# The attention mask moves from a TensorE product to a GpSimd addition, and the one-element copy in front of VectorE's score step goes

## The chip, the cores and the metric

One Trainium2 chip, one of its cores. The metric is the device time of one execution in microseconds (us). The engines are called PE (TensorE, with PEld for its weight loads), DVE (VectorE), ACT (ScalarE), POOL (GpSimd) and SP (SyncE, which here only issues transfers).

## The reference

Sixteen sequences (a batch each) of 512 tokens with 512 features pass through a chain: a finite-difference step on a 512x512 field, then a transformer layer, then an adapter with two 2x2 rotations. Only the transformer layer matters here, and of it the attention:

```python
scores = jnp.einsum('bhqd,bhkd->bhqk', q / math.sqrt(HEAD_DIM), k)
scores = scores + attention_bias
scores = jnp.where(src_mask, -jnp.inf, scores.astype(jnp.float32))
probs = jax.nn.softmax(scores, axis=-1).astype(v.dtype)
ctx = jnp.einsum('bhqk,bhkd->bhqd', probs, v)
```

There are 16 heads of 32 features. The bias is 16 x 16 x 512 x 512 float32 (268 MB in all) and is read once; the mask is one byte per query and key, the same for all heads of a batch. After the attention come the output product, a layer norm, a feed-forward part with 2048 hidden units, and the adapter.

## The kernel before

**Tiles and stages.** The kernel goes through the 16 batches one after the other. Within a batch the attention works in four groups g = 0..3. A group holds four heads (HG = 4) and all four blocks of 128 queries (TB = 4), so it has 16 score blocks of 128 queries by 512 keys, numbered i = 4q + j. A score block i of a group lives in `prob[:, i, :]` from the landing of its bias to its turn. All products with large matrices are split into high and low parts in float32r; the low part of a weight is computed by POOL (`split_lo`, line 628) from the raw weight and the high part that ACT copied (`split_hi`, line 689), and PE waits for it through `w_lo`.

**One score block.** PE multiplies query and key parts into one of two PSUM banks (L915), and a second matmul with a bfloat16 identity adds the mask rows `mask_add` to the same bank (L916). DVE copies one element (`fence`, L1117; that instruction carries the waits for the scores and for the bias in `prob`), and then one custom instruction computes score plus bias negated into `prob` with its row minimum into `low` (L1118). ACT takes the exponential and the row sum (L698). PE turns the block in four 128x128 pieces (L927), ACT copies the turned block to `probT` (L719), and PE multiplies every four of them with V (L950).

**Order of the work.** Every engine has its order written out by hand. Iteration i of a group on PE issues the score block i + 7 (`S_LEAD` = 7, running over into the next group), then turns block i, then some pieces of the query and key product for the group after the next (`qk_piece`, L891; in groups 0 and 1 from i = 5 on), and at i = 1, 5, 9, 13 the product with V. ACT takes in iteration i the exponential of block i + 6 (`EXP_LEAD` = 6), then the copy of block i; at i = 14 of a group this is the exponential of block 4 of the next group. DVE takes the score step i + 7 and, in the first four iterations, the steps that make the next group's query and key: L1098 and L1096 (from PSUM to `wide`) and the two L1103 (low parts: `wide` minus `parts`, both in SBUF).

**SP's queue** decides when transfers start. In each of groups 0 to 2, SP issues after the turns of blocks 1 and 3 two bias loads for the next group (each 512 KB: two blocks of `prob`, `load_bias`, L531). It then waits for both L1103 (`qk_lo`) and issues the 16 small transfers that lay out query and key for the next group (`load_stack`, L536). Only then come the bias loads for blocks 4 to 15 of the next group, each after the turn of the second block whose place it takes. PE's score block 0..3 of the next group (iterations 9 to 12) waits for its four `load_stack` transfers. In the feed-forward part, SP loads weight chunks and, between them, the bias of the next batch's group 0.

**POOL's queue** before the change: per batch 24 low parts of weights (L628), three additions of a bias row to 128x2048 tiles (L650 in group 0, L664, L676) and 12 small roots (L633). In the attention it holds few instructions: in group 0 the low part for group 2's weights and then L650, at the start of group 1 the low part for group 3's weights, at the start of group 2 that of the first half of the output weights, in group 3 that of their second half.

**The feed-forward part** goes over 16 chunks f. For each one PE makes the hidden units (12 matmuls), ACT applies the activation into `gel` (L810) and copies the high part (L814), DVE makes the low part (L1197, both inputs in SBUF), and PE makes the second product (12 matmuls) after the first product of the next chunk. At f = 8, 10, 12 and 14 DVE also scales a quarter of the next input in `adapt`: L1067, L1080 and L1081, each waiting for the one in front of it. ACT makes the high part of chunk f + 3 at the end of its chunk f, and POOL follows with the low part.

Of the kernel before, what the change touches and what calls it, by code (L numbers as in the profile page):

```python
# [18 lines left out]
BF16 = mybir.dt.bfloat16  # L19
U8 = mybir.dt.uint8  # L20
I32 = mybir.dt.int32
ALU = mybir.AluOpType
# [390 lines left out]
def layers(nc, keep, x1, mask, bias, ada_rows, sel_turned, Wq, bq, Wk, bk, Wv, bv, Wo, bo, W1, b1, W2, b2, g2, beta2,  # L413
# [3 lines left out]
    with ExitStack() as ctx:  # L417
# [19 lines left out]
        mask_eye = sb("mask_eye", [P, P], BF16)  # L437
# [41 lines left out]
        eye_ready, score_full, scored, exped, inv_ready, inverted = (  # L479
            sem(n) for n in ("eye_ready", "score_full", "scored", "exped", "inv_ready", "inverted"))  # L480
# [21 lines left out]
        with nc.Block() as block:  # L502

            @block.sync
            def _(sp):
                for signal in (*w_hi, *w_lo, *proj_full, *proj_read, probT_full, tok_ready, mask_ready, mixed, ff2_done,
                               pv_done, g_lo, turn_lo, scored, *turned_copied, ctx_scaled, out_ready):
                    sp.sem_inc(signal, START)
# [112 lines left out]
            def _(pool):  # L621
# [13 lines left out]
                pool.wait_ge(keep["ident_in"], 16)  # L635
                pool.tensor_copy(mask_eye[:], ident[:]).then_inc(eye_ready, 1)
# [6 lines left out]

                pool.wait_ge(consts_in, 16 * 12)
                for b in range(0, B):
# [5 lines left out]
                    for g in (1, 2):  # L651
                        split_lo(0, ITEMS[0] * b + W0_QK + g + 2)
# [13 lines left out]

                    for f in range(6, NF):
                        split_lo(*chunk_item(b, f // 4, f % 4))
                        if more and f < 6 + TB:
                            root(ROOTS * b + 2 * TB + f - 5, f - 6)  # L670
# [169 lines left out]
            def _(t):  # L840
# [68 lines left out]
                def score_block(b, g, i):  # L909
# [5 lines left out]
                    t.matmul(score[i % 2][:], stack[g % 2][:, j, 0, q * P:(q + 1) * P], stack[g % 2][:, j, 1, :], start=True, stop=False)  # L915
                    t.matmul(score[i % 2][:], mask_eye[:], mask_add[:, q, :], start=False, stop=True).then_inc(score_full, 1)  # L916
# [55 lines left out]
                t.wait_ge(eye_ready, 1)  # L972
# [3 lines left out]
                for b in range(0, B):  # L976
                    t.wait_ge(mask_ready, b + 1 + START)
# [76 lines left out]
            def _(v):  # L1054
# [14 lines left out]
                def number_mask(b):  # L1069

                    v.wait_ge(mask_in, 16 * (b + 1))
                    v.tensor_scalar(mask_add[:], mask8[:], MASKED, None, ALU.mult).then_inc(mask_ready, 1)
# [39 lines left out]
                def score_step(b, g, i):  # L1112

                    v.wait_ge(score_full, 64 * b + 16 * g + i + 1)
                    if i % 2 == 0:
                        v.wait_ge(bias_in[i // HG][i % HG // 2], 16 * (4 * b + g + 1))
                    v.tensor_copy(fence[:, i % 7:i % 7 + 1], cur[:, 0:1])  # L1117
# [219 lines left out]
```

## Time and profile before

| what | before |
|---|---|
| time, median of 3 runs | 4866.53 us (4855.59 to 4870.71) |
| profiled execution | 4863.62 us, of it a span of 4861.2 us between first and last instruction |
| busy in the span | PE 88%, PEld 63%, DVE 54%, ACT 51%, POOL 26% |
| mean granted TensorE clock | 0.945 of full speed |
| moved by DMA | 704.31 MB, mean 145 GB/s |

In the rows below, a timeline row gives the start, the duration, the engine, the line of the kernel, the operation, written and read tile names, shapes and count; what stands in square brackets is the idle time of that engine just before the row and what ended it. A group row (by line) gives busy time and the mean duration of one, then the idle time before them. A duration of an instruction that had to wait after it was issued holds that wait too. In the windows, what follows the stretch and its length is the busy time (and instructions) of PE, PEld, DVE, ACT and POOL, then the granted TensorE clock, the DMA share and GB/s. Batches are counted from 0. L12 is line 12 of the kernel before.

### The profile page before, as it was taken

How to read it: one execution, taken by the hardware profiler on the slowest of the kernel's cores; microseconds unless marked ns; L12 is line 12 of the kernel's file. 1: busy time of each engine (PE TensorE's matmuls, PEld its weight loads, DVE VectorE, ACT ScalarE, POOL GpSimd, SP SyncE). 2: the span in 40 equal slices, each digit the busy share in tenths (PEclk: the TensorE clock that was granted, in tenths of full speed). 3: DMA queues.
4: the chain of work that ended last, by engine and by line, in shares of the span. 5: the costliest groups of instructions: out<-in, count | busy, mean ns of one | idle time of the engine just before them, and what ended most of it. 6: DMA issues, size and time to landing. Idle time of an engine off the chain costs nothing.

```text
span 4861.2 us, 70568 instructions
## 1 busy us (share of the span) xinstructions
PE 4253.7 (88%) x25568; PEld 3038.8 (63%) x25808; DVE 2612.4 (54%) x5783; ACT 2489.6 (51%) x4700; POOL 1272.4 (26%) x637
## 2 busy tenths in 40 slices
PE   6996688898989898888989898888989898988887
PEld 3441466676767666666767676666767676666665
DVE  8991545545463646455454646455454636455553
ACT  0002464737474555647374655647374746546472
POOL 0000132231414232231414142332314142322313
PEclk9995899999999999999999999999999999999999
DMA  3223653636364554536364644536363645545361
GB/s 120 105 97 67 200 172 106 192 109 183 124 195 132 162 164 118 178 105 193 115 182 136 188 144 138 169 107 191 109 183 124 195 132 162 163 113 182 108 181 48
DMA packets 534759, 704.31 MB, mean 145 GB/s; under 512 B 45280, under 2 KB 254992, under 8 KB 534384
## 3 DMA queue, kind: packets, MB, share of 16 engines
q1 hardware_dynamic: 517520, 666.23, 46.2%
q10 hardware_dynamic: 16896, 33.56, 1.8%
q8 instruction: 209, 3.42, 0.3%
q14 instruction: 134, 1.10, 0.1%
HBM read 529.30 MB, written 35.72 MB: 116 GB/s over the span
## 4 chain that ended last, share of the span: by engine, by line
PE 54%; DVE 12%; SPq 7%; ACT 6%; issue 5%; DMA 3%; POOL 3%; another core or an unknown queue 0%; POOLq 0%; DVEq 0%; ACTq 0%
PE bank L846 33%; SPq L536 7%; PE bank L891 5%; PE bank L927 5%; PE bank L915 3%; PE bank L950 3%; DVE prob L1118 2%; PE bank L916 2%; DMA stack<-parts 2%; DVE parts L1197 1%; ACT probT L719 1%; DMA V<-in_L_cond_W 1%; DVE parts L1103 1%; ACT prob L698 1%; PE bank L855 1%
## 5 line engine op out<-in xcount | busy, mean ns | idle before, releaser
L628 POOL TENSOR_TENSOR w<-w_raw,w 128x1024 fp32r<-128x1024 f32 x240 | 587.7, 2449 | 2067.0 <-ACT w L689 1935.7
L698 ACT ACTIVATE prob<-prob,low 128x512 f32<-128x512 f32 x1024 | 736.6, 719 | 171.8 <-DVE low L1118 171.8
L1197 DVE TENSOR_TENSOR parts<-gel,parts 128x512 fp32r<-128x512 f32 x256 | 261.3, 1021 | 893.7 <-ACT parts L814 893.7
L719 ACT ACTIVATE probT<-bank 128x512 f32<-128x512 f32 x1024 | 608.8, 595 | 248.7 <-PE bank L927 234.0
L927 PE MATMUL bank<-ident,prob 128*128 128x128 f32 x4096 | 641.1, 280 | 96.3 <-ACT probT L719 70.4
L1118 DVE CUSTOM_DVE_ANT_0 prob<-bank,prob 128x512 f32<-128x512 f32 x1024 | 696.3, 680 | 0.0
L927 PEld LDWEIGHTS bank<-ident,prob 128*128 128x128 f32 x4096 | 504.2, 145 | 204.3 <-issue 77.8
L915 PE MATMUL bank<-stack 128*128 128x512 f32 x1024 | 485.5, 476 | 105.0 <-DMA stack<-parts 58.2
L1117 DVE COPY fence<-cur 128x1 f32<-128x1 f32 x1024 | 155.5, 152 | 676.8 <-PE bank L916 334.9
L846 PE MATMUL bank<-xT,stack 128*128 128x512 f32 x1920 | 491.5, 405 | 23.1 <-DVE xT L1089 12.0
L628 POOL TENSOR_TENSOR stack<-V,stack 128x1024 fp32r<-128x1024 f32 x144 | 353.0, 2454 | 596.2 <-ACT stack L689 592.5
L891 PE MATMUL bank<-xT,w 128*128 128x512 f32 x1152 | 421.9, 469 | 62.5 <-POOL w L628 62.5
L846 PEld LDWEIGHTS bank<-xT,stack 128*128 128x128 f32 x1920 | 361.1, 192 | 138.6 <-DVE xT L1089 32.4
L810 ACT ACTIVATE gel<-bank,b_col 128x512 f32<-128x512 f32 x256 | 176.5, 690 | 505.7 <-PE bank L846 505.7
L846 PE MATMUL bank<-xT,w 128*128 128x512 f32 x1536 | 379.7, 396 | 0.0
L689 ACT ACTIVATE w<-w_raw 128x1024 fp32r<-128x1024 f32 x240 | 253.9, 1058 | 244.7 <-PE bank L846 222.1
L846 PE MATMUL bank<-w,parts 128*128 128x512 f32 x1536 | 372.1, 393 | 6.3 <-DVE parts L1197 6.3
L846 PE MATMUL bank<-stack,parts 128*128 128x512 f32 x1536 | 373.5, 392 | 0.0
L846 PE MATMUL bank<-w,xT 128*128 128x512 f32 x1536 | 369.4, 398 | 1.9
L846 PEld LDWEIGHTS bank<-w,parts 128*128 128x128 f32 x1536 | 287.0, 188 | 77.6 <-DVE parts L1197 13.3
L846 PEld LDWEIGHTS bank<-w,xT 128*128 128x128 f32 x1536 | 286.0, 188 | 78.8 <-DVE xT L1129 8.9
L846 PEld LDWEIGHTS bank<-xT,w 128*128 128x128 f32 x1536 | 288.1, 188 | 68.7
(182 smaller groups left out, 5881.9 us busy)
## 6 DMA issues: line engine op xcount, KB each, us to landing
prob<-in_fside_Bx16xSxS SPq DMA_DIRECT2D x512, 512.0 KB, 4.9
stack<-parts SPq DMA_DIRECT2D x1024, 128.0 KB, 2.5
V<-in_L_cond_W SPq DMA_DIRECT2D x256, 256.0 KB, 3.7
w_raw<-in_L_cond_W SPq DMA_DIRECT2D x256, 256.0 KB, 3.0
field<-in_x SPq DMA_DIRECT2D x16, 1024.0 KB, 5.3
x<-total ACTq DMA_DIRECT2D x16, 1024.0 KB, 5.9
xin<-x SPq DMA_DIRECT2D x16, 1024.0 KB, 5.6
w_raw<-in_L_cond_Wv SPq DMA_DIRECT2D x64, 256.0 KB, 2.9
```

What stands on the lines that cost most here:

```text
L536: sp.dma_start(stack[g % 2][DH * quad:DH * (quad + 1), j, :, :].bitcast(F32), parts[DH * j:DH * (j + 1), q:q + step + 1:step, :].bitcast(F ...
L628: pool.tensor_tensor(w[s][:, 1, :], w_raw[s], w[s][:, 0, :].bitcast(F32), ALU.subtract).then_inc(w_lo[s], 1)
L689: act.activation(w[s][:, 0, :], w_raw[s], ACT.Copy).then_inc(w_hi[s], 1)
L698: act.activation(prob[:, i, :], prob[:, i, :], ACT.Exp, bias=low[:, i:i + 1], scale=-1.0, accum_out=total[:, g % 2, i:i + 1]).then_inc(exp ...
L719: act.activation(probT[:, i % 8, :], turned[e % 2][:], ACT.Copy).then_inc(turned_copied[e % 2], 1)
L810: act.activation(gel[:, s, :], proj[s][:], ACT.Gelu_apprx_sigmoid, bias=col["b1"][:, f:f + 1]).then_inc(proj_read[s], 1)
L846: mm = t.matmul(dst, stat(hs, k), mov(hm, k), start=start and n == 0, stop=stop and n == count - 1)
L891: mm = t.matmul(proj[c][:], weight(0, hs)[:, KB * c + k, :], xT[hm][:, k, :], start=n == 0, stop=n == len(QK_TERMS) - 1)
L915: t.matmul(score[i % 2][:], stack[g % 2][:, j, 0, q * P:(q + 1) * P], stack[g % 2][:, j, 1, :], start=True, stop=False)
L927: mm = t.transpose(turned[e % 2][:, k * P:(k + 1) * P], prob[:, i, k * P:(k + 1) * P], ident[:])
L1118: v.tensor_tensor_reduce(prob[:, i, :], score[i % 2][:], prob[:, i, :], -1.0, MIN_START, ALU.add, ALU.min, low[:, i:i + 1]).then_inc(score ...
L1197: v.tensor_tensor(parts[:, 2 * (f % 2) + 1, :], gel[:, f % 2, :], parts[:, 2 * (f % 2), :].bitcast(F32), ALU.subtract).then_inc(g_lo, 1)
```

## The change

The mask is no longer added by PE. POOL adds it to the bias in SBUF, in `prob`, as soon as the bias has landed and before DVE reads it: one instruction for the two blocks of one bias load (128 x 1024), so 8 in each group and 32 in a batch. The second matmul of a score block, the identity that it needed and PE's waits for it go. DVE's score step waits for POOL (`bias_masked`) in place of the landing of the bias, and the one-element copy in front of it goes, so that the waits stand directly at the custom instruction. The making of `mask_add` waits in addition until the previous batch's mask additions are done.

The additions for groups 1, 2 and 3 stand in POOL's queue behind L650, behind the low part for group 3's weights, and behind the low part of the first half of the output weights. Those for group 0 of the next batch stand behind the low parts of chunks 8 to 15, one behind each. The copies of turned probabilities (L719) all run on ScalarE before the change too; the diff doesn't touch them.

```diff
             def _(pool):
+                def add_mask(b, g, q, halves=(0, 1)):
+                    for h in halves:
+                        pool.wait_ge(bias_in[q][h], 16 * (4 * b + g + 1))
+                        half = prob[:, HG * q + 2 * h:HG * q + 2 * h + 2, :]
+                        pool.tensor_tensor(half, half, mask_add[:, q:q + 1, :].to_broadcast([P, 2, S]), ALU.add).then_inc(bias_masked, 1)
...
-                pool.wait_ge(keep["ident_in"], 16)
-                pool.tensor_copy(mask_eye[:], ident[:]).then_inc(eye_ready, 1)
...
+                pool.wait_ge(mask_ready, 1 + START)
+                for q in range(TB):
+                    add_mask(0, 0, q)
                 pool.wait_ge(consts_in, 16 * 12)
                 for b in range(0, B):
...
                     pool.tensor_tensor(xin[:], xin[:], bcast(row["bo"]), ALU.add).then_inc(xin_biased, 1)
-                    for g in (1, 2):
-                        split_lo(0, ITEMS[0] * b + W0_QK + g + 2)
+                    for g in (0, 1, 2):
+                        if g:
+                            split_lo(0, ITEMS[0] * b + W0_QK + g + 2)
+                        for q in range(TB):
+                            add_mask(b, g + 1, q)
...
+                    if more:
+                        pool.wait_ge(mask_ready, b + 2 + START)
                     for f in range(6, NF):
                         split_lo(*chunk_item(b, f // 4, f % 4))
+                        if more and f >= 8:
+                            add_mask(b + 1, 0, (f - 8) // 2, (f % 2,))
...
             def _(t):
-                    t.matmul(score[i % 2][:], stack[g % 2][:, j, 0, q * P:(q + 1) * P], stack[g % 2][:, j, 1, :], start=True, stop=False)
-                    t.matmul(score[i % 2][:], mask_eye[:], mask_add[:, q, :], start=False, stop=True).then_inc(score_full, 1)
+                    t.matmul(score[i % 2][:], stack[g % 2][:, j, 0, q * P:(q + 1) * P], stack[g % 2][:, j, 1, :], start=True, stop=True).then_inc(score_full, 1)
...
-                t.wait_ge(eye_ready, 1)
+                t.wait_ge(keep["ident_in"], 16)
...
-                    t.wait_ge(mask_ready, b + 1 + START)
...
             def _(v):
                     v.wait_ge(mask_in, 16 * (b + 1))
+                    v.wait_ge(bias_masked, 32 * b + START)
                     v.tensor_scalar(mask_add[:], mask8[:], MASKED, None, ALU.mult).then_inc(mask_ready, 1)
...
                     if i % 2 == 0:
-                        v.wait_ge(bias_in[i // HG][i % HG // 2], 16 * (4 * b + g + 1))
-                    v.tensor_copy(fence[:, i % 7:i % 7 + 1], cur[:, 0:1])
+                        v.wait_ge(bias_masked, 32 * b + 8 * g + i // 2 + 1 + START)
                     v.tensor_tensor_reduce(prob[:, i, :], score[i % 2][:], prob[:, i, :], -1.0, MIN_START, ALU.add, ALU.min,
                                            low[:, i:i + 1]).then_inc(scored, 1)
```

## Rows read from the trace of the kernel before

**Rows 1.** Windows of batch 2: group 1, group 2, group 3, the feed-forward part.
```profile
1127.00:1154.00 27.00, 25.55 (x249) 18.16 (x252) 15.61 (x55) 22.60 (x53) 2.39 (x1) 1.00 0.86 254
1154.00:1181.00 27.00, 22.79 (x223) 15.97 (x226) 16.21 (x56) 21.84 (x52) 2.39 (x1) 0.87 0.81 233
1181.00:1206.00 25.00, 22.05 (x260) 16.04 (x261) 10.78 (x35) 20.95 (x45) 2.38 (x1) 1.00 0.15 47
1226.00:1313.00 87.00, 86.32 (x372) 69.68 (x373) 29.08 (x46) 36.84 (x47) 42.83 (x20) 1.00 0.40 131
```

**Rows 2.** PE's timeline, one iteration of group 1 without the product with V.
```profile
1137.04 0.39 PE L915 MATMUL bank<-stack 128*128 128x512 f32 x1
1137.28 0.39 PE L916 MATMUL bank<-mask_add,mask_eye 128*128 128x512 bf16 x1
1137.50 0.60 PE L927 MATMUL bank<-ident,prob 128*128 128x128 f32 x4
```

**Rows 3.** SP's timeline in group 1: the stack, then three bias loads.
```profile
1132.73 11.01 SPq L536 DMA_DIRECT2D stack<-parts  x16
1143.78 1.65 SPq L531 DMA_DIRECT2D prob<-in_fside_Bx16xSxS  x3
```

**Rows 4.** PE's timeline: the last stack of groups 1 and 2 awaited.
```profile
1145.78 0.47 PE L915 MATMUL bank<-stack 128*128 128x512 f32 x1 [0.52 <-DMA stack<-parts]
...
1173.52 0.77 PE L915 MATMUL bank<-stack 128*128 128x512 f32 x1 [1.16 <-DMA stack<-parts]
```

**Rows 5.** Line 531, issue at 1143.8 alone: issue and time to landing.
```profile
L531 SPq DMA_DIRECT2D prob<-in_fside_Bx16xSxS x1: 593/593/593, 1143.8 to 1143.8; - x1
DMA to landing us min/median/max: 3.7/3.7/3.7
```

**Rows 6.** DVE and ACT: score step and exponential of group 2's block 4, the copy after.
```profile
1147.89 0.15 DVE L1117 COPY fence<-cur 128x1 f32<-128x1 f32 x1 [0.61 <-PE bank L916]
1147.96 0.68 DVE L1118 CUSTOM_DVE_ANT_0 prob<-bank,prob 128x512 f32<-128x512 f32 x1
...
1148.82 0.71 ACT L698 ACTIVATE prob<-prob,low 128x512 f32<-128x512 f32 x1
...
1150.91 0.60 ACT L719 ACTIVATE probT<-bank 128x512 f32<-128x512 f32 x1 [1.28 <-PE bank L927]
```

**Rows 7.** Group 0: POOL's long addition beside DVE's first low part.
```profile
1098.08 4.53 POOL L650 TENSOR_TENSOR xin<-xin,bo_row 128x2048 f32<-128x2048 f32 x1
1098.40 4.75 DVE L1103 TENSOR_TENSOR parts<-wide,parts 128x512 fp32r<-128x512 f32 x1
```

**Rows 8.** Group 1: POOL's low part beside DVE, and the two L1103.
```profile
1127.67 2.39 POOL L628 TENSOR_TENSOR w<-w_raw,w 128x1024 fp32r<-128x1024 f32 x1 [25.06 <-ACT w L689]
...
1128.40 0.68 DVE L1118 CUSTOM_DVE_ANT_0 prob<-bank,prob 128x512 f32<-128x512 f32 x1
...
1130.69 0.69 DVE L1103 TENSOR_TENSOR parts<-wide,parts 128x512 fp32r<-128x512 f32 x1
...
1131.97 0.69 DVE L1103 TENSOR_TENSOR parts<-wide,parts 128x512 fp32r<-128x512 f32 x1
```

**Rows 9.** Feed-forward, chunks 8 and 9: POOL, DVE and the product that needs L1197.
```profile
1268.01 2.40 POOL L628 TENSOR_TENSOR w<-w_raw,w 128x1024 fp32r<-128x1024 f32 x1
1271.06 0.69 DVE L1197 TENSOR_TENSOR parts<-gel,parts 128x512 fp32r<-128x512 f32 x1 [3.80 <-ACT parts L814]
1271.67 0.54 DVE L1067 TENSOR_SCALAR xin<-xin,agg,rstd 128x512 f32<-128x512 f32 x1
1273.57 2.40 POOL L628 TENSOR_TENSOR w<-w_raw,w 128x1024 fp32r<-128x1024 f32 x1 [3.16 <-ACT w L689]
1280.60 0.63 PE L846 MATMUL bank<-stack,parts 128*128 128x512 f32 x2
```

**Rows 10.** End of a batch: POOL behind DVE's run of two-input instructions.
```profile
1348.20 6.45 DVE L1258 SCALAR_TENSOR_TENSOR res<-res,cur,tok 128x512 f32<-128x512 f32 x4
1350.91 2.77 POOL L628 TENSOR_TENSOR w<-w_raw,w 128x1024 fp32r<-128x1024 f32 x1 [15.18 <-ACT w L689]
```

More of the change, by code:

```diff
@@ L436, in layers @@
         sel_T = sb("sel_T", [A, A])
-        mask_eye = sb("mask_eye", [P, P], BF16)
         cur = sb("cur", [P, 8])
@@ L478, in layers @@
         qk_hi, qk_lo = sem("qk_hi"), sem("qk_lo")
-        eye_ready, score_full, scored, exped, inv_ready, inverted = (
-            sem(n) for n in ("eye_ready", "score_full", "scored", "exped", "inv_ready", "inverted"))
+        bias_masked, score_full, scored, exped, inv_ready, inverted = (
+            sem(n) for n in ("bias_masked", "score_full", "scored", "exped", "inv_ready", "inverted"))
         probT_full, pv_done, ctx_scaled = (sem(n) for n in ("probT_full", "pv_done", "ctx_scaled"))
@@ L506, in _ @@
                 for signal in (*w_hi, *w_lo, *proj_full, *proj_read, probT_full, tok_ready, mask_ready, mixed, ff2_done,
-                               pv_done, g_lo, turn_lo, scored, *turned_copied, ctx_scaled, out_ready):
+                               pv_done, g_lo, turn_lo, scored, *turned_copied, ctx_scaled, bias_masked, out_ready):
                     sp.sem_inc(signal, START)
```

## Prediction

> **What bounds the kernel now.** I read the page first: in a span of 4861.2 us PE is busy 88%, ACT 51%, DVE 54% and POOL 26%. That says that work taken off PE should pay, and that POOL has room. Both have to be read stage by stage, so I next took the windows of one batch [rows 1]. In the feed-forward part PE is busy 86.3 of 87.0 us; nothing but PE counts there, as long as the others keep up. Group 1 is nearly full on PE (25.6 of 27.0) and ACT is not far behind (22.6). Group 2 has no product pieces to fill PE, yet takes the same 27 us: something other than PE sets its length.
>
> The timeline of SP shows what it is [rows 3]. The 16 stack transfers are issued one by one from 1132.73, which takes 11.0 us, and only then come the bias loads for blocks 4 and up of the next group. PE waits for the last stack in both groups, 0.52 and 1.16 us [rows 4]. The first bias load behind them, issued at 1143.8, lands 3.7 us later, at 1147.5 [rows 3, 5], and DVE's score step for that block begins at 1147.89 [rows 6]. So the bias arrives 0.4 us before its use. This chain (the two L1103, SP's 11 us, the landing, the score step, ACT's exponential at 1148.82) runs beside PE's work in groups 0 to 2 and has almost no slack. ACT idles 1.28 us before the copy that follows [rows 6]; that is all a late exponential can eat before the next turn waits.
>
> **The change, part by part.**
>
> *The mask matmul.* On PE the next instruction starts 0.22 to 0.24 us after it or its neighbour [rows 2], so its price is 0.23 us and not its recorded 0.39. Over 1024 blocks that is 235 us, the most this edit could give. Seven of them per batch stand ahead of group 0, between product pieces that keep PE full: 7 x 0.23 = 1.6 us, and I take 2.0 because two run while PE has only just restarted at half its clock after a wait (as the first row after the wait in group 2, 0.77 against 0.47 [rows 4]). Nine stand in group 3 (2.1 us), where ACT is busy 21 of 25 us [rows 1] and paces the second half: I take 1.0. The other 48 lie in groups 0 to 2, where the chain above decides.
>
> *The one-element copy.* The custom instruction starts 0.07 us after it [rows 6]. In the first five score steps of a group, which DVE does back to back with the low parts, this brings the chain 0.3 us forward. Elsewhere DVE waits for PE, and it is worth nothing. The most would be its mean 0.15 us each, the least nothing.
>
> *The additions on POOL.* The trace has no bfloat16 broadcast addition. The nearest rows are L628, same 1024 float32 elements, 2.39 and 2.40 us [rows 8, 9], and L650, a broadcast row over 2048, 4.53 us [rows 7], again 2.3 for 1024. I take 2.4; a cheaper second operand could not save more than a part of it, and I see no reason for more. 32 of them in a batch are 77 us of POOL, about as much as it did before.
>
> First cost: they lie in the chain. The bias of block 4 is ready at 1147.5 + 2.4 = 1149.9 and not at 1147.5.
>
> Second cost: DVE and POOL block each other. L1103 normally takes 0.69 us; where it starts at 1098.40, beside L650 (1098.08 to 1102.61), it takes 4.75 and ends 0.5 us after it [rows 7]. L1118, which reads one input from PSUM, takes 0.68 us beside a running L628 [rows 8]. So an instruction with two inputs in SBUF waits for POOL's whole instruction, and the score step doesn't. POOL waits the same way: at 1350.91 an L628 takes 2.77, and the four L1258 beside it 6.45 us where four of 1.4 would be 5.7 [rows 10]; POOL got in between two of DVE's. This is what the Trainium skill (SBUF — State Buffer, "SBUF: two separate sides") calls an exclusive lock: whichever starts first has the shared pair for its whole instruction and the other fully blocks. The trace agrees (4.75 us). By that rule the sum is the one below; without it the rival with no collisions would be the forecast.
>
> Where do the additions run? Loads for blocks 4 to 9 are issued together at 1143.8 to 1145.4 [rows 3] and those up to 15 follow as turns allow. POOL needs 2.4 us each, six in a row, so from about 1147.5 it is busy without a break until some 8 to 10 us into the next group, with group 3's weights queued behind in group 1. The two L1103 come 3.5 to 5 us into a group, the first at 1130.69 and the second at 1131.97 [rows 8]. The first falls into an addition: half a length, 1.2 us. Then POOL takes the next addition, DVE does a score step (0.7), and the second L1103 waits for the rest: 2.4 - 0.7 = 1.7. Together 2.9 us later to SP.
>
> Group 1 and group 2: 2.9 - 0.3 (copy) + 2.4 (addition) = 5.0 later at the score step, less the slack of 0.4 and ACT's 1.28: **+3.3 us** for group 1, and I take 3.0 for group 2, where PE already waits for the stack for 1.16 us and some of the delay is in the time of before. Group 0: its first L1103 waits for L650 already, so only the second is new: 1.7 - 0.3 + 2.4 - 0.4 - 1.3 = **+2.1 us**. The wait of PE for group 3's low weights (POOL gives them about 3 us later than PE asks) lies before the chain's end and is hidden by it. Attention: -2.0 + 2.1 + 3.3 + 3.0 - 1.0 = +5.4 us a batch, 16 batches: **+86 us**.
>
> *Feed-forward.* Behind the low part that starts at 1268.01 comes an addition, 1270.4 to 1272.8. L1197 of chunk 8 wants to start at 1271.06 and ends at 1273.5; there is time, for each chunk's low part is needed some 4 us after its usual start (chunk 9: 1276.62 by the same 5.56 us step, needed at 1280.60) [rows 9]. But chunk 8 also has L1067, L1080 and L1081, each a wait of its own. L1067 to 1273.9; POOL's next low part, ready at 1273.57, 1273.9 to 1276.3; L1080 to 1277.0; POOL's addition to 1279.4; L1081 to 1280.1; POOL's low part, ready at 1279.13, to 1282.5; L1197 of chunk 9 to 1283.2. PE needs it at 1280.60: **2.6 us** late, in a stage without slack. The same can come in chunks 10 and 12. After one stall the phases shift, so I take one and a half per batch: 3.9 x 15 batches = **+58 us** (bounds: none, and three with the lower clock after each).
>
> Outside these, POOL's queue is no longer than before: its additions for group 3 end before ACT has the second half of the output weights ready. The first batch's eight additions come while the first products run; nothing is counted.
>
> Sum: 4863.6 (this profiled execution) + 86 + 58 = 5008 us. The median of the runs is 2.9 us above that execution, which I leave out.
>
> **The rivals.**
>
> *Collisions only in the attention* (the low part L1197 follows L1081 at once, because POOL doesn't get in between). 4863.6 + 86 = 4950 us. For it: L1197's four microseconds of room hold one addition. Against: rows 10 show POOL getting in.
>
> *No collisions* (the L1103 fall between additions, or POOL doesn't hold DVE up). Each of groups 0 to 2 then pays 2.4 - 0.3 - 0.4 - 1.3 = 0.4 us; -2.0 - 1.0 + 1.2 = -1.8 a batch, 16 batches: 29 us, 4835 us, faster than before. It decides where the two L1103 of a group together wait less than about 0.6 us. Against it: rows 7.
>
> *Half the collisions*: about 1.5 us a group less, 3 x 1.5 x 16 = 72, and no stall in the feed-forward part: 4950 - 72 = 4878 us, no difference.
>
> *The chain isn't binding* and PE gives all it is relieved of: 4864 - 235 = 4629 us. Against it: PE's waits for the stack in groups 1 and 2 [rows 4], and the 27 us of group 2.
>
> *POOL over-full in the feed-forward part*: three stalls of 2.6 us, each followed by some microseconds at half the clock (as in rows 4), say 5 us each, 15 x 15 = 225 us, and the attention's 86: 5175 us.
>
> **How the numbers follow.** Forecast (near 5008) 0.36, attention only (4950) 0.25, over-full (5175) 0.12, half (4878) 0.09, no collisions (4835) 0.15, chain not binding (4629) 0.03. The range from 4815 to 5110 leaves out the last and the over-full case, 0.15; the likeliest case's own range is 4965 to 5050. Within 0.3% (15 us; about what a measurement of this kernel can tell) lies most of the half case and an edge of the no-collision one: 0.07. Faster 0.20, slower 0.73.
>
> **What the profile after would show.** PE: no L916 row, and between scores and turn 0.23 us less. POOL: 512 additions of 2.4 us, busy about 52%. DVE: the mean of L1103 up from 1193 ns to about 2.5 us, of L1197 up from 1021, L1118 unchanged at 0.68. SP: the stack's first issue after the second L1103, some 2.6 us later within groups 1 and 2; these groups near 30 us, group 3 near 24. PE waits for the low part in chunks 9, 11 or 13. The prediction is wrong if L1103 stays near its mean (then 4835), if an addition takes well under 2.4 us, or if groups 1 and 2 shorten by 3 us (then the chain never bound).

## The result, and the profile after

The changed kernel took 4919.72 us (median of 4 runs, 4919.3 to 4932.69), the kernel before 4861.06 us beside it. The ratio is 1.0125, with a 95% interval from 1.0099 to 1.0151: slower by some 59 us. The forecast was 5008 us, slower by 144. The direction was right and the time lies in the stated range, but the loss is less than half of the forecast (59 against 144 us).

In the changed kernel the lines of the code are numbered anew: L1103 is L1115, L628 is L627, L650 is L656, L891 is L904, L915 is L928, L1118 is L1129, L1197 is L1208, L1067 is L1078, and L1080 and L1081 are L1092 and L1093. The two lines whose starts bound the stages below, L915 and L935 before, are L928 and L947. The addition is L638. First the page after (the engines' busy time, then its costliest groups):

```profile
PE 4097.2 (83%) x24784; PEld 2987.7 (61%) x24784; DVE 2914.2 (59%) x4759; ACT 2466.1 (50%) x4700; POOL 2452.7 (50%) x1148
...
L638 POOL TENSOR_TENSOR prob<-prob,mask_add 128x1024 f32<-128x1024 f32 x512 | 1151.4, 2271 | 448.0 <-DMA prob<-in_fside_Bx16xSxS 448.0
...
L1208 DVE TENSOR_TENSOR parts<-gel,parts 128x512 fp32r<-128x512 f32 x256 | 419.6, 1644 | 650.0 <-ACT parts L827 650.0
...
L928 PE MATMUL bank<-stack 128*128 128x512 f32 x1024 | 489.9, 481 | 138.5 <-DMA stack<-parts 106.9
...
L904 PE MATMUL bank<-xT,w 128*128 128x512 f32 x1152 | 417.8, 467 | 121.9 <-POOL w L627 121.9
```

PE lost 157 us of busy time (4253.7 to 4097.2), and POOL gained 1180, and yet the kernel is slower: PE's idle time in the span grew by 213 us. L1208 has the same work as L1197 before and takes 1644 ns where it took 1021. The low parts of query and key went the same way, 1193 to 1740 ns. The groups by line, first of the kernel before:

```profile
L1197 DVE TENSOR_TENSOR parts<-gel,parts 128x512 fp32r<-128x512 f32 x256 | 261.3, 1021 | 893.7 <-ACT parts L814 893.7
L915 PE MATMUL bank<-stack 128*128 128x512 f32 x1024 | 485.5, 476 | 105.0 <-DMA stack<-parts 58.2 <-DVE low L1118 46.0
L1103 DVE TENSOR_TENSOR parts<-wide,parts 128x512 fp32r<-128x512 f32 x128 | 152.7, 1193 | 1.6
```

and of the kernel after:

```profile
L1129 DVE CUSTOM_DVE_ANT_0 prob<-bank,prob 128x512 f32<-128x512 f32 x1024 | 695.4, 688 | 660.5 <-PE bank L928 519.5 <-POOL prob L638 140.1
L1115 DVE TENSOR_TENSOR parts<-wide,parts 128x512 fp32r<-128x512 f32 x128 | 222.8, 1740 | 1.7
```

Not all of the loss is where the forecast put it, and that shows in a table by stage. I took the start of the turn of the scales (L935 before, i = 14 of each group) and the first score matmul of a batch from PE's timeline, and took means over the 15 batches that have a successor (us):

| stretch of a batch | before | after | difference |
|---|---|---|---|
| first scores to group 0's scales | 44.2 | 41.5 | -2.7 |
| to group 1's | 27.1 | 29.8 | +2.6 |
| to group 2's | 27.6 | 28.7 | +1.1 |
| to group 3's | 19.6 | 20.5 | +0.9 |
| to the next batch's first scores (output product, feed-forward, adapter) | 151.2 | 152.8 | +1.6 |
| batch | 269.7 | 273.3 | +3.6 |

**Group 1 of batch 2** on the timelines of DVE, PE and POOL of the kernel after, beside [rows 8]:

```profile
1133.53 1.33 DVE L1115 TENSOR_TENSOR parts<-wide,parts 128x512 fp32r<-128x512 f32 x1
1135.39 2.01 DVE L1115 TENSOR_TENSOR parts<-wide,parts 128x512 fp32r<-128x512 f32 x1
...
1141.84 1.19 PE L904 MATMUL bank<-xT,w 128*128 128x512 f32 x2 [4.09 <-POOL w L627]
```

```profile
1132.16 7.23 POOL L638 TENSOR_TENSOR prob<-prob,mask_add 128x1024 f32<-128x1024 f32 x3 [1.30 <-DMA prob<-in_fside_Bx16xSxS]
1139.35 2.34 POOL L627 TENSOR_TENSOR w<-w_raw,w 128x1024 fp32r<-128x1024 f32 x1
```

POOL runs three additions without a break, and both low parts fall into them: 0.6 and 1.3 us of waiting each beyond their 0.69. Behind them in POOL's queue stands the low part of group 3's weights, and PE waits 4.1 us for it.

**Chunks 8 and 9 of the feed-forward part** in the kernel after, on the timelines of DVE, POOL and PE, beside [rows 9]:

```profile
1277.68 0.93 DVE L1208 TENSOR_TENSOR parts<-gel,parts 128x512 fp32r<-128x512 f32 x1 [3.44 <-ACT parts L827]
1278.02 2.60 POOL L638 TENSOR_TENSOR prob<-prob,mask_add 128x1024 f32<-128x1024 f32 x1
1278.53 2.38 DVE L1078 TENSOR_SCALAR xin<-xin,agg,rstd 128x512 f32<-128x512 f32 x1
1280.58 2.59 POOL L627 TENSOR_TENSOR w<-w_raw,w 128x1024 fp32r<-128x1024 f32 x1
1280.94 2.77 DVE L1092 TENSOR_TENSOR xin<-xin,scale_row 128x512 f32<-128x512 f32 x1
1283.12 2.60 POOL L638 TENSOR_TENSOR prob<-prob,mask_add 128x1024 f32<-128x1024 f32 x1
1283.75 2.52 DVE L1093 TENSOR_TENSOR xin<-xin,shift_row 128x512 f32<-128x512 f32 x1
1285.74 2.75 POOL L627 TENSOR_TENSOR stack<-V,stack 128x1024 fp32r<-128x1024 f32 x1
1286.19 5.41 DVE L1208 TENSOR_TENSOR parts<-gel,parts 128x512 fp32r<-128x512 f32 x2
1289.10 3.01 PE L859 MATMUL bank<-stack,parts 128*128 128x512 f32 x12 [1.73 <-DVE parts L1208]
```

The two engines take turns, each held up by the other's instruction, much as the prediction walked it through. Two things differ: L1208 of chunk 8 was hardly held (0.93 us), and L1078, which the prediction let pass, was. PE is late in chunk 9, by 1.73 us in this batch, and so it is once in each of the 15 batches that have a successor (1.73 to 1.76 us).

### The profile page after: what moved, and what is told of

The parts are those of the page before. It is cut to its first block, busy times and chain, and to the rows that moved or that the text cites. A ratio compares the mean times of both kernels' runs of the same rounds, so it can differ in the third digit from the quotient of the medians.

```text
span 4917.5 us, 68280 instructions
## 1 busy us (share of the span) xinstructions
PE 4097.2 (83%) x24784; PEld 2987.7 (61%) x24784; DVE 2914.2 (59%) x4759; ACT 2466.1 (50%) x4700; POOL 2452.7 (50%) x1148
## 4 chain that ended last, share of the span: by engine, by line
PE 42%; DVE 14%; ACT 8%; SPq 7%; POOL 6%; DMA 6%; issue 6%; DVEq 0%; POOLq 0%; ACTq 0%
PE bank L859 29%; SPq L535 7%; PE bank L904 4%; DMA prob<-in_fside_Bx16xSxS 3%; DVE parts L1115 3%; PE bank L939 3%; POOL prob L638 3%; DVE parts L1208 2%; PE bank L962 2%; ACT prob L711 2%; PE bank L928 2%; POOL w L627 2%; ACT probT L732 2%; DMA stack<-parts 2%; DMA V<-in_L_cond_W 1%
## 5 line engine op out<-in xcount | busy, mean ns | idle before, releaser
L638 POOL TENSOR_TENSOR prob<-prob,mask_add 128x1024 f32<-128x1024 f32 x512 | 1151.4, 2271 | 448.0 <-DMA prob<-in_fside_Bx16xSxS 448.0
L1129 DVE CUSTOM_DVE_ANT_0 prob<-bank,prob 128x512 f32<-128x512 f32 x1024 | 695.4, 688 | 660.5 <-PE bank L928 519.5
L627 POOL TENSOR_TENSOR w<-w_raw,w 128x1024 fp32r<-128x1024 f32 x240 | 613.5, 2556 | 651.1 <-ACT w L702 521.2
L939 PE MATMUL bank<-ident,prob 128*128 128x128 f32 x4096 | 653.7, 285 | 186.2 <-ACT probT L732 178.8
L1208 DVE TENSOR_TENSOR parts<-gel,parts 128x512 fp32r<-128x512 f32 x256 | 419.6, 1644 | 650.0 <-ACT parts L827 650.0
L928 PE MATMUL bank<-stack 128*128 128x512 f32 x1024 | 489.9, 481 | 138.5 <-DMA stack<-parts 106.9
L627 POOL TENSOR_TENSOR stack<-V,stack 128x1024 fp32r<-128x1024 f32 x144 | 358.9, 2495 | 492.9 <-ACT stack L702 490.5
L904 PE MATMUL bank<-xT,w 128*128 128x512 f32 x1152 | 417.8, 467 | 121.9 <-POOL w L627 121.9
L928 PEld LDWEIGHTS bank<-stack 128*128 128x128 f32 x1024 | 204.5, 200 | 242.4 <-issue 147.9
L859 PEld LDWEIGHTS bank<-stack,parts 128*128 128x128 f32 x1536 | 287.3, 188 | 97.4 <-DVE parts L1208 32.6
```

The source lines that it names most:

```text
L627: pool.tensor_tensor(w[s][:, 1, :], w_raw[s], w[s][:, 0, :].bitcast(F32), ALU.subtract).then_inc(w_lo[s], 1)
L638: pool.tensor_tensor(half, half, mask_add[:, q:q + 1, :].to_broadcast([P, 2, S]), ALU.add).then_inc(bias_masked, 1)
L859: mm = t.matmul(dst, stat(hs, k), mov(hm, k), start=start and n == 0, stop=stop and n == count - 1)
L904: mm = t.matmul(proj[c][:], weight(0, hs)[:, KB * c + k, :], xT[hm][:, k, :], start=n == 0, stop=n == len(QK_TERMS) - 1)
L939: mm = t.transpose(turned[e % 2][:, k * P:(k + 1) * P], prob[:, i, k * P:(k + 1) * P], ident[:])
L1129: v.tensor_tensor_reduce(prob[:, i, :], score[i % 2][:], prob[:, i, :], -1.0, MIN_START, ALU.add, ALU.min, low[:, i:i + 1]).then_inc(score ...
```

## The experiments

Each time below is a median of 4 to 6 runs with the ratio to runs of the kernel before on the same chip (its medians there were 4856 to 4865 us).

### The mask matmul alone, and the copy

```diff
-                    t.matmul(score[i % 2][:], stack[g % 2][:, j, 0, q * P:(q + 1) * P], stack[g % 2][:, j, 1, :], start=True, stop=False)
-                    t.matmul(score[i % 2][:], mask_eye[:], mask_add[:, q, :], start=False, stop=True).then_inc(score_full, 1)
+                    t.matmul(score[i % 2][:], stack[g % 2][:, j, 0, q * P:(q + 1) * P], stack[g % 2][:, j, 1, :], start=True, stop=True).then_inc(score_full, 1)
```

> The kernel before with the mask matmul left out and nothing in its place (this leaves the mask out of the computation). It gives the price of that matmul alone. If the chain of low parts, stack transfers and bias loads holds groups 1 and 2 (the prediction's step), only the stretch up to group 0's end and a little of the rest shorten: some 3 us up to the end of group 0, 0.5 to 1 in each of groups 1 to 3, 5 us a batch, 4861 - 80 = 4780 us. If PE is the bound throughout the attention (rival), nearly all of 1024 x 0.23 us comes back: 4640 us.

Measured: 4807.16 us, 0.9877 (0.9860 to 0.9893), 57 us less than before. So a quarter of the 235 us comes back. It is less than the 80 us expected: by the stage table the stretch to group 0's scales gave 2.4 us and groups 1 and 2 gave 0.5 and 0.4, but group 3 became 0.4 us longer. PE's wait for the stack transfers grew from 58.2 to 90.5 us in the groups by line:

```profile
L915 PE MATMUL bank<-stack 128*128 128x512 f32 x1024 | 488.1, 479 | 137.6 <-DMA stack<-parts 90.5 <-DVE low L1117 46.7
```

The second run takes the copy out as well.

```diff
-                    v.tensor_copy(fence[:, i % 7:i % 7 + 1], cur[:, 0:1])
```

> As the run without the mask matmul, and the one-element copy goes too, so that the waits stand at the custom instruction. If the copy only costs where DVE works back to back (five score steps of each of groups 0 to 2, 0.07 us each), 3 x 0.3 x 16 = 15 us less than that run at most, 4765 us. If each copy were on the path with its 0.15 us, 150 us less. If the custom instruction pays for holding the waits itself, no change or slower. What the kernel after is above this run is the price of the POOL additions.

Measured: 4781.51 us, 0.9826 (0.9808 to 0.9844), 26 us less than the run with the copy, somewhat above the 15 expected; the custom instruction takes 689 ns instead of 680 where it holds the waits itself. Together the two removals are worth 83 us. The kernel after is 138 us above this run (145 by the two ratios to the kernel before, for these two were not run side by side): that is the price of the additions, and what follows asks how it comes about.

### The additions without anybody waiting for them

```diff
+                def add_mask(b, g, q, halves=(0, 1)):
+                    for h in halves:
+                        pool.wait_ge(bias_in[q][h], 16 * (4 * b + g + 1))
+                        pool.wait_ge(bias_masked, 32 * b + 8 * g + 2 * q + h + START)
+                        pool.tensor_tensor(tok[:, 0:2, :], tok[:, 2:4, :], mask_add[:, q:q + 1, :].to_broadcast([P, 2, S]), ALU.add).then_inc(bias_masked, 1)
...
```

The calls stand where the changed kernel has them. The tile `tok` is free at these times, and some added waits keep it so: POOL waits for the end of the previous batch's output, and VectorE waits for the last addition before it writes `tok` again. The mask matmul and the copy stay, so the comparison is with the kernel before.

> The kernel before (mask matmul and copy kept) with the 512 POOL additions at the same places of POOL's queue and after the same landings, but read from and written to another tile, so that nobody waits for their result. It has the lock between POOL and DVE and the longer POOL queue without the added step in the chain. If lock and queue do the harm: 23 us from the feed-forward part and 2 to 3 us a batch from the attention, 4925 to 4935 us. If the harm is only that DVE waits for each addition: no change, 4861 us.

Measured: 5006.32 us, 1.0289 (1.0267 to 1.0311), 142 us above the kernel before. The loss is as large as that of the real additions (138) though no score step waits for a result. By the stage table it lies in the same places: group 1 +4.1, group 2 +1.9, the last stretch +1.4, beside +3.6, +1.9 and +1.7 for the real ones (the kernel after against the run without mask and copy). Only group 3 differs, +0.1 against +0.7. The low parts of query and key are slow again, as beside the real additions:

```profile
L1123 DVE TENSOR_TENSOR parts<-wide,parts 128x512 fp32r<-128x512 f32 x128 | 246.1, 1923 | 1.6
```

So lock and POOL's queue do most of the harm. It came out higher than the 64 to 74 us I expected. The control is not a perfect one: the low parts took 1923 ns here and 1740 beside the real additions, so the lock cost more, and a small part of the real loss may still be VectorE's wait for the addition. In group 3 it is.

### POOL's queue alone

```diff
-                        if g:
+                        if g == 2:
                             split_lo(0, ITEMS[0] * b + W0_QK + g + 2)
                         for q in range(TB):
+                            if g == 0 and q == 3:
+                                split_lo(0, ITEMS[0] * b + W0_QK + 3)
                             add_mask(b, g + 1, q)
```

> The changed kernel with one instruction moved in POOL's queue: the low part of group 3's weights goes ahead of the last two mask additions of group 1 (those of blocks 12 to 15). In the changed kernel PE waited 121.9 us in all for POOL's low parts at that line, against 62.5 before. If this wait is on the path, the 59 us go or most of them: 4865 to 4880 us. If it is hidden by the chain of stack transfers, as the prediction had it: 4919 us, no change.

Measured: 4932.74 us, 1.0143 (1.0122 to 1.0163): no gain over the kernel after. The edit does what it says, and the wait goes elsewhere, as the groups by line show (PE's wait for POOL from 121.9 to 69.8, its wait for the stack from 106.9 to 144.5):

```profile
L930 PE MATMUL bank<-stack 128*128 128x512 f32 x1024 | 493.6, 484 | 173.9 <-DMA stack<-parts 144.5 <-DVE low L1131 28.0
...
L906 PE MATMUL bank<-xT,w 128*128 128x512 f32 x1152 | 413.3, 462 | 69.8 <-POOL w L627 69.8
```

Group 1 is only 0.6 us shorter (29.8 to 29.1): the wait for the low weights is hidden behind the stack, as the prediction had said. The median is even 13 us above that of the kernel after (the intervals overlap), and the last stretch is 154.6 us against 152.8. PE's timeline in chunk 9 of batch 3 shows a part of the reason: after the wait the same twelve matmuls take 4.61 us, where in batch 2 they take 3.02.

```profile
1563.51 4.61 PE L861 MATMUL bank<-stack,parts 128*128 128x512 f32 x12 [1.77 <-DVE parts L1210]
```

The windows right behind the two waits differ in the granted clock, 0.69 in batch 3 and 1.00 in batch 2. It was 0.69 behind this wait in 9 of the 15 batches; in the kernel after, where the wait was 1.73 to 1.76 us and not 1.77, it was 1.00 in all 15.

```profile
1563.00:1568.50 5.50, 5.00 (x15) 3.94 (x16) 4.84 (x5) 0.47 (x2) 2.44 (x1) 0.69 0.39 122
...
1291.50:1296.00 4.50, 3.80 (x17) 3.12 (x18) 4.43 (x5) 1.07 (x2) 2.65 (x2) 1.00 0.59 186
```

### The lock in front of the stack transfers

```diff
+                        if g > 1:
+                            t.wait_ge(qk_lo, 8 * b + 2 * (g - 1) + c + 1)
...
-                    v.tensor_tensor(parts[:, 2 * c + 1, :], wide[:, c, :], parts[:, 2 * c, :].bitcast(F32), ALU.subtract).then_inc(qk_lo, 1)
+                    low_part, high = parts[:, 2 * c + 1, :], parts[:, 2 * c, :].bitcast(F32)
+                    if g == 0:
+                        v.tensor_tensor(low_part, wide[:, c, :], high, ALU.subtract).then_inc(qk_lo, 1)
+                    elif c:
+                        v.scalar_tensor_tensor(low_part, proj[1][:], col["bk"][:, g:g + 1], high, ALU.add, ALU.subtract).then_inc(qk_lo, 1)
+                    else:
+                        v.scalar_tensor_tensor(low_part, proj[0][:], QSCALE, high, ALU.mult, ALU.subtract).then_inc(qk_lo, 1)
...
```

> The changed kernel, but in groups 1 to 3 the low parts of query and key are made from the product in PSUM and not from its copy in SBUF, so that these two VectorE instructions have one input in SBUF only (for the query the low part leaves out the bias bq, which is zero in these inputs). If the lock between POOL and VectorE in front of the stack transfers is what the additions cost in the attention, these instructions fall from 1.74 us to about 0.75, SP's stack begins 2 us earlier in groups 1 and 2 and 3 us earlier in group 0: 2 + 2 + 1 to 3 us a batch, 4920 - 80 to 110 = 4810 to 4840 us. If the additions cost through POOL's longer queue or through VectorE's wait for them, nothing changes: 4920 us.

Measured: 4839.16 us, 0.9956 (0.9939 to 0.9973), 80 us below the kernel after and a little faster than before (0.4%). The expectation is wrong about the inputs: bq is not zero in them (it is drawn with a spread of 0.8), so this kernel leaves the query's bias out of the scores of groups 1 to 3. Its time is of use, but it is not a complete kernel. By the stage table the stretch to group 0's scales fell from 41.5 to 37.7 us and group 2 from 28.7 to 26.0, but group 1 only from 29.8 to 29.4. PE still waited 97.1 us for POOL's low weights. In group 1 two delays lie side by side, and to take away either of them alone gives about half a microsecond.

Not all of the 80 us are the additions' doing. The gain in the first stretch, 3.8 us a batch, is the lock with L650, which was there before the change; the last runs of this section show that. What belongs to the additions here is group 2's 2.7 us. And this run loses 1.9 us a batch in the last stretch (154.7 us), where the granted clock behind the wait of chunk 9 was again 0.69 in 9 of 15 batches.

### The feed-forward part

```diff
-                        if more and f >= 8:
-                            add_mask(b + 1, 0, (f - 8) // 2, (f % 2,))
+                        if more and f in (8, 9, 10, 12, 14):
+                            n = (8, 9, 10, 12, 14).index(f)
+                            add_mask(b + 1, 0, n // 2, (n % 2,))
...
+                        for n in (5, 6, 7):
+                            add_mask(b + 1, 0, n // 2, (n % 2,))
                         split_lo(2, ITEMS[2] * (b + 1) + W2_QK0)
```

> The changed kernel with the eight additions of the feed-forward part placed otherwise: behind the low parts of chunks 8, 9, 10, 12 and 14, and three behind that of chunk 15, so that none stands beside the two-input instructions that scale the next input. If PE's wait for the low part of chunk 9 comes from these collisions, as the prediction had it, the stretch from group 3's end to the next batch loses its 1.5 us: 4920 - 24 = 4896 us. If that stretch is longer for another reason, 4920 us.

Measured: 4887.83 us, 1.0062 (1.0047 to 1.0077), 32 us below the kernel after. The last stretch is 151.5 us, as before the change, and the matmuls of that form, which waited 26.0 us in all for DVE's low parts in the kernel after, wait for nothing:

```profile
L862 PE MATMUL bank<-stack,parts 128*128 128x512 f32 x1536 | 373.5, 392 | 0.0
```

### A bias load ahead of the last stack

```diff
                             for j in range(HG):
+                                if j == 3:
+                                    sp.wait_ge(probT_full, ENTRIES * b + entry(g, 5) + 1 + START)
+                                    load_bias(b, g + 1, 1, 0)
                                 load_stack(b, g + 1, j)
+                            continue
```

> The changed kernel with one transfer moved in SP's queue: the bias load of blocks 4 and 5 goes ahead of the last four of the 16 stack transfers, 2.6 us earlier. If the addition lengthens the chain from that landing to ScalarE's exponential (the prediction's 2.4 us step), 1 to 1.5 us a group come back: 4920 - 60 = 4860 us. If not (the additions to an idle tile cost as much as the real ones, which speaks for the lock alone), no change or, by the stack that lands 0.6 us later, up to 30 us slower.

Measured: 5077.84 us, 1.0448 (1.0432 to 1.0463), 158 us slower than the kernel after, and neither theory expected that. DVE's wait for POOL's additions did fall, from 140.1 to 17.9 us. PE's wait for the stack rose from 106.9 to 249.1 us, 142 more, which is most of the loss:

```profile
L932 PE MATMUL bank<-stack 128*128 128x512 f32 x1024 | 505.2, 496 | 273.2 <-DMA stack<-parts 249.1 <-DVE low L1133 22.5
```

The four small transfers behind the 512 KB one come late. In batch 2's group 0, SP had issued them by 1147.65, and the matmul that needed them began at 1151.26, 3.6 us later, where the median landing of a stack transfer is 2.4 in the kernel after. In the mean over the batches, the slowest of the last four transfers landed 4.2 to 4.3 us after its issue in this run, and 2.6 to 3.2 in the kernel after; their issue behind the first twelve came 0.6 us later, which is the issue of the load itself and no wait of SP's.

```profile
1145.12 2.53 SPq L535 DMA_DIRECT2D stack<-parts  x4
```

```profile
1151.26 0.47 PE L932 MATMUL bank<-stack 128*128 128x512 f32 x1 [2.40 <-DMA stack<-parts]
```

So the order of before, small ones first, is the better one, and the stack is the half of the chain that matters more. The next run had this edit as well, and the query low part without its bias.

> The last three edits together, and the low part of group 3's weights ahead of the additions of blocks 12 to 15. If the lock is the cost: 4920 - 80 to 110 - 24 and PE's 52 us of waits for the low part of the weights, which would be on the path once the stack comes early: 4790 us or so, near the kernel without any mask (4782) and faster than before. If the lock is not the cost: 4890 us or above.

Measured: 4897.37 us, 1.0085 (1.0068 to 1.0103). That is in the range for "the lock is not the cost", but PE waited 188.2 us for the stack, against 56.6 in the run with the PSUM low parts alone. I took the early bias load for the reason and tried the other edits without it.

### The edits that held, together, and their control

The last three kernels write query and key with their biases back to their PSUM bank, so that nothing is left out of the low parts; ScalarE reads the bank too:

```diff
-                    act.activation(parts[:, 2 * c, :], wide[:, c, :], ACT.Copy).then_inc(qk_hi, 1)
+                    act.activation(parts[:, 2 * c, :], proj[c][:] if g else wide[:, c, :], ACT.Copy).then_inc(qk_hi, 1)
...
+                    dst = proj[c][:] if g else wide[:, c, :]
                     if c:
-                        ins = v.tensor_scalar(wide[:, 1, :], proj[1][:], bias_col, None, ALU.add)
+                        ins = v.tensor_scalar(dst, proj[1][:], bias_col, None, ALU.add)
                     else:
-                        ins = v.tensor_scalar(wide[:, 0, :], proj[0][:], bias_col, QSCALE, ALU.add, ALU.mult)
+                        ins = v.tensor_scalar(dst, proj[0][:], bias_col, QSCALE, ALU.add, ALU.mult)
...
-                    v.tensor_tensor(parts[:, 2 * c + 1, :], wide[:, c, :], parts[:, 2 * c, :].bitcast(F32), ALU.subtract).then_inc(qk_lo, 1)
+                    v.tensor_tensor(parts[:, 2 * c + 1, :], proj[c][:] if g else wide[:, c, :], parts[:, 2 * c, :].bitcast(F32), ALU.subtract).then_inc(qk_lo, 1)
...
+                        if g > 1:
+                            t.wait_ge(qk_lo, 8 * b + 2 * (g - 1) + c + 1)
...
```

> The changed kernel with three edits: in groups 1 to 3 the query and key with their biases are written back to their PSUM bank, so that both low parts read one input from PSUM (nothing is left out now); the additions of the feed-forward part stand away from the scaling of the next input; the low part of group 3's weights stands ahead of the additions of blocks 12 to 15. By the stage times of the runs with one edit each: 37.7 up to the end of group 0, 29.4 - 1.7 in group 1 (PE's wait for the low weights is now on the path), 26.0, 21.1, and 151.2 to the next batch, 263.7 us a batch against 269.7 of the kernel before: 4861 - 96 = 4765 us. If the waits move somewhere else: 4820 us, what the first two edits give alone.

Measured: 4760.2 us, 0.9795 (0.9779 to 0.9812), near the 4765 expected. This is the fastest complete kernel of the study, 2.0% below the kernel before. The low parts take their plain time, in the groups by line of this kernel:

```profile
L1124 DVE TENSOR_TENSOR parts<-bank,parts 128x512 fp32r<-128x512 f32 x96 | 66.0, 687 | 1.1 <-ACT parts L756 0.6
```

Group 1 is 26.7 us: beside the run with the feed-forward edit alone (29.7) that is 3.0 less for two edits that gave 0.4 and 0.6 one by one (the first of them in its other form, without the write to PSUM).

> The kernel before with only that query and key are written back to PSUM. It gets nothing from the mask's move. If the lock matters before the change too, it is L650 in group 0 against the first L1103: 4.1 us a batch, of which 2.5 to 4 are on the path: 4861 - 40 to 64 = 4800 to 4820 us. If that wait is hidden, 4861 us.

Measured: 4792.12 us, 0.9867 (0.9852 to 0.9882), 65 us less for an edit that has nothing to do with the mask, and a little more than expected. The stretch to group 0's scales fell from 44.2 to 39.3 us, and no other changed by more than 0.4: the wait in [rows 7] (4.75 us for an instruction of 0.69, so 4.1) was on the path all along. The mean granted clock of this stretch also rose, from 0.87 to 0.94, so the stretch gained more than the wait.

> The kernel without mask matmul and without copy (the mask is left out of the computation), with query and key written back to PSUM. It is the floor for any way to add the mask that costs nothing. 4782 less what the lock costs there in group 0 (2.5 to 4 us a batch): 4720 to 4742 us. What the run with the additions and all three edits is above it is what POOL's additions still cost: by the forecasts 25 to 45 us.

Measured: 4721.54 us, 0.9723 (0.9709 to 0.9738). The kernel with additions and all edits is 39 us above this floor, against 138 us for the kernel after above its own. By stretch these are 0.4, 0.6, 0.0, 1.2 and 0.0 us a batch: more than half of what is left lies in group 3.

## Why the prediction was right or wrong, step by step

*What binds the attention.* Right. The mask matmul gave back 57 us of 235, and PE's wait for the stack grew by 32. The rival in which PE gives all it is relieved of (4629) is out.

*What the two removals save.* Forecast 3.0 us a batch outside the chain and 0.3 us in each of three groups, 3.9 in all; measured 4.6 (269.7 to 265.1 in the stage table of the run without both). The total is near, but the terms are not: group 3 was to give 1.0 and lost 0.2, and groups 1 and 2 gave 0.9 and 0.8 and not 0.3.

*The lock as the cause.* Right, and shown from two sides: additions whose result no score step waits for cost 142 us, and the price of the real ones falls from 138 to 39 us when the low parts read PSUM, the additions of the feed-forward part stand elsewhere (32 us of this) and one low part of weights moves ahead. This is the rule of the Trainium skill (SBUF — State Buffer, "SBUF: two separate sides"), and the trace after agrees with it (a low part took 4.45 us beside POOL's L656 of 5.04, and 0.69 alone). The rival with no collisions is out. One row was read too low: the four L1258 of [rows 10] would take 4.3 us undisturbed (the same four, L1269, take 4.30 in batch 2 of the kernel after) and not 5.7, so POOL held them up by some 2 us. The sum did not use it.

*The sizes.* Here the prediction failed. The step that is wrong is the sum of what the collisions cost, and in it the terms of group 0, group 2 and the feed-forward part. The sum had 13 us a batch for the additions: 9.3 in the attention (the net 5.4 with the 3.9 of savings added back) and 3.7 in the feed-forward part. The kernel after is 8.2 us a batch above the run without mask and copy: 6.5 in the attention and 1.7 behind it. By term:

- **Group 0, forecast +2.4 for the additions (+2.1 with the copy), measured +0.3.** I let the first low part wait for L650 and the second for an addition. Without mask matmul and copy, DVE comes to its first low part 0.08 us before POOL starts its long addition, and POOL is the one that waits. Only the second low part is held, and by the same instruction as before. So it is in every batch but the first. The idle additions, which keep mask matmul and copy, did give the picture of the forecast (first low part 4.6 us, second 1.95 in the mean), and even there this stretch grew by only 0.4 us. The two engines' rows of the kernel after:

```profile
1103.24 0.69 DVE L1115 TENSOR_TENSOR parts<-wide,parts 128x512 fp32r<-128x512 f32 x1
1104.45 4.45 DVE L1115 TENSOR_TENSOR parts<-wide,parts 128x512 fp32r<-128x512 f32 x1
```

```profile
1103.32 5.04 POOL L656 TENSOR_TENSOR xin<-xin,bo_row 128x2048 f32<-128x2048 f32 x1
```

- **Group 1, forecast +3.6, measured +3.6**, but not by the forecast's sum: that the numbers meet is luck. The two low parts waited 2.0 us in batch 2, not 2.9. In addition PE waited 4.1 us for the low weights, and I had called that hidden. It is hidden as long as the stack is late too: each of the two alone holds the group, which is why neither edit helped by itself. A third part is the clock: PE's idle time in group 1 is 2.0 us longer than in the run without mask and copy, and its mean granted clock there is 0.92, against 0.98 in that run and 1.00 before. The forecast had no term for that.
- **Group 2, forecast +3.3, measured +1.9.** Here there is no second delay. The low parts are 2.1 us a batch longer than in the run without mask and copy, and the loss is gone when they read PSUM (26.7 us, as the floor).
- **The 2.4 us of the addition within the chain** was in the sums of groups 0 to 2. The idle additions, without that wait, cost as much there as the real ones (+0.4, +4.1 and +1.9 against +0.3, +3.6 and +1.9), and with the lock out of the way these groups are 1.0 us a batch above the floor together. So the term was small, though how small is not shown: the idle additions met a somewhat stronger lock.
- **Group 3, forecast 1.0 saved, measured 0.9 lost.** Of this 0.2 is there without the additions, and 0.7 comes with them. Idle additions cost only 0.1 here, and with the lock gone the real ones cost 1.2. VectorE's idle time in this group that POOL's additions end is 1.9 us a batch (2.5 with all edits). So here the wait for the addition itself costs, in the one group of the attention where the forecast gave the additions no price.
- **Feed-forward, forecast +58 us, measured +23** (1.55 us a batch over 15 batches). The first stall came where the walk-through put it, in chunk 9. It was 1.7 us and not 2.6. From the time that the low part of chunk 8 could start to the end of chunk 9's, the walk-through has 12.1 us (1271.06 to 1283.2), the trace 11.4 (1277.68 to 1289.05). It let POOL start every 3.1 to 3.5 us; in the rows POOL starts every 2.5 to 2.6 us (1278.02, 1280.58, 1283.12, 1285.74). An addition that nobody holds up takes 2.15 us and not 2.4, and the rows of the two engines overlap by some tenths at each turn; how much each of the two gives is not separated. The stall came once a batch and not one and a half times: chunk 10's low part was held as well (1288.97 to 1291.60), but PE did not wait for it.

Two rivals had a better size than the forecast: collisions in the attention alone (4950) and half the collisions (4878). Neither is what happened, for both have no stall in the feed-forward part, and there was one in each batch. The attention lost less than the first said and more than the second. Nor did POOL become over-full (5175).

## What to carry to other kernels

POOL with room on the page is not POOL with room for everybody: an addition moved there has to be laid against every VectorE instruction that reads its operands from SBUF, and those on a latency chain (here in front of 16 transfers) should read one operand from PSUM if they can. That was worth 65 us without any other change. Together with two changes of order in POOL's queue it turned the mask's move from a loss of 59 us into a gain of 32 (4792 to 4760). Where two delays end at the same place, an experiment that removes one shows next to nothing; remove both before calling either harmless. And where a collision decides, an order that hangs on a tenth of a microsecond should widen the forecast and not be summed.

## What the runs showed of the hardware that I had not expected

- A VectorE instruction with a single input in SBUF also waited for POOL: the TENSOR_SCALAR at 1278.53 took 2.38 us, beside the POOL addition of 1278.02, where its like before took 0.54 [rows 9].
- The addition with a bfloat16 broadcast as its second input is faster than one of two float32 tiles of the same size, 2.15 us in the median against 2.40 for L628 [rows 9]:

```profile
L638 POOL TENSOR_TENSOR prob<-prob,mask_add x512: 2120/2148/2612, 544.7 to 4747.9; 128x1024 f32<-128x1024 f32 x171
```

- One 512 KB load put ahead of the last four 128 KB transfers in SP's queue made PE wait 142 us more over the run, though the issue of these four moved by only 0.6 us behind the first twelve.
- After the same wait of 1.77 us in chunk 9, PE went on with a granted clock of 0.69 in 9 batches and of 1.00 in 6 others of the same execution (the run with one low part of weights ahead of the additions).
